# Moving the turn of x behind the value products in a pipelined transformer block

## The reference

```
tgt1 = layer_norm(tgt, g1, be1)
q, k, v = tgt1 @ Wq.T + bq, tgt1 @ Wk.T + bk, tgt1 @ Wv.T + bv
p = softmax(q k^T / 4 + (1 - mask) * -1e9)        # 16 heads
tgt = tgt + (p v) @ Wo.T + bo + memory @ Wg.T + bg
tgt1 = layer_norm(tgt, g2, be2)
return tgt + relu(tgt1 @ W1.T + b1) @ W2.T + b2
```

## Time and profile before

| | us |
|---|---|
| median of 3 runs | 1762.45 (1761.9 to 1763.15) |
| the profiled execution | 1762.95 |
| its span | 1761.2 |
| PE busy | 1723.3 (98%) |
| ScalarE busy | 1435.8 (82%) |
| VectorE busy | 1323.8 (75%) |
| GpSimd busy | 800.4 (45%) |

### The profile page before, as it was taken

How to read it: one execution, slowest core, us unless ns; L and a number is a source line. 1 busy time by engine, 2 the same in 40 slices (tenths; PEclk the granted TensorE clock), 3 DMA queues, 4 the chain that set the end, 5 groups by cost and what they waited for, 6 DMA issues and landing times.

```text
span 1761.2 us, 53553 instructions
## 1 busy us (share of the span) xinstructions
PE 1723.3 (98%) x17780; PEld 1696.0 (96%) x17780; DVE 1323.8 (75%) x6935; ACT 1435.8 (82%) x5577; POOL 800.4 (45%) x782
## 2 busy tenths in 40 slices
PE   5899999999999999999999999999999999999997
PEld 5799999999999999999999999999999999999997
DVE  7677777777777777777777777787777777777772
ACT  4888888888888888888888888888888888888882
POOL 4244444444444444444454454444444444444444
PEclk8899999999999999999999999999999999999999
DMA  5333333333333333333333333332433433433320
GB/s 169 109 127 107 115 123 108 117 121 107 120 121 106 121 120 107 122 118 109 121 118 103 127 112 105 131 118 95 134 116 96 135 113 100 134 112 103 126 80 25
DMA packets 185796, 200.46 MB, mean 114 GB/s; under 512 B 18864, under 2 KB 135984, under 8 KB 185520
## 3 DMA queue, kind: packets, MB, share of 16 engines
q1 hardware_dynamic: 185520, 197.02, 34.0%
HBM read 62.73 MB, written 16.78 MB: 45 GB/s over the span
## 4 chain that ended last, share of the span: by engine, by line
PE 95%; ACT 2%; DVE 1%; issue 0%; SPq 0%; DMA 0%; ACTq 0%; DVEq 0%
PE ffn_ps L808 13%; PE ffn_ps L810 13%; PE ffn_ps L809 13%; PE turn_ps L874 12%; PE work_ps L808 9%; PE work_ps L810 8%; PE work_ps L809 8%; PE score_ps L860 7%; PE value_ps L897 7%; PE work_ps L825 3%; ACT scores L388 1%; PE turn_ps L882 0%; ACT probs L400 0%; DVE xhat L556 0%; ACT hid L430 0%
## 5 line engine op out<-in xcount | busy, mean ns | idle before, releaser
L388 ACT ACTIVATE scores<-scores,row_min 128x128 f32<-128x128 f32 x2048 | 795.1, 402 | 2.3 <-DVE row_min L624 2.2
L738 POOL TENSOR_TENSOR hT_lo<-hid,hT_hi 128x512 fp32r<-128x512 f32 x256 | 355.0, 1387 | 511.9 <-DVE hT_hi L651 511.9
L624 DVE CUSTOM_DVE_ANT_0 scores<-score_ps,mask_bias 128x128 f32<-128x128 f32 x2048 | 472.4, 286 | 3.3 <-issue 2.9
L400 ACT ACTIVATE probs<-turn_ps 128x512 f32<-128x512 f32 x512 | 304.1, 595 | 163.0 <-PE turn_ps L874 163.0
L388 ACT ACTIVATION_READ_ACCUMULATOR scores<-scores,row_min 128x1 f32 x2048 | 411.1, 201 | 0.0
L874 PE MATMUL turn_ps<-ident,scores 128*128 128x128 f32 x2048 | 308.2, 273 | 5.3 <-ACT probs L400 5.2
L808 PE MATMUL ffn_ps<-zT_hi,w_lo 128*128 128x256 f32 x1024 | 302.2, 295 | 5.2 <-ACT hid L430 4.0
L808 PE MATMUL ffn_ps<-w_hi,hT_lo 128*128 128x256 f32 x1024 | 300.7, 294 | 2.4 <-ACT hid L430 2.4
L809 PE MATMUL ffn_ps<-zT_lo,w_hi 128*128 128x256 f32 x1024 | 285.5, 279 | 0.0
L810 PE MATMUL ffn_ps<-zT_hi,w_hi 128*128 128x256 f32 x1024 | 285.0, 278 | 0.0
L810 PE MATMUL ffn_ps<-w_hi,hT_hi 128*128 128x256 f32 x1024 | 284.7, 278 | 0.0
(11 more groups left out here) (112 smaller groups left out, 4187.1 us busy)
## 6 DMA issues: line engine op xcount, KB each, us to landing
q_stack<-q_hi SPq DMA_DIRECT2D x128, 256.0 KB, 2.4
k_stack<-k_hi SPq DMA_DIRECT2D x256, 128.0 KB, 2.3
x_in<-x_dram SPq DMA_DIRECT2D x64, 256.0 KB, 2.7
mem_in<-memory_dram SPq DMA_DIRECT2D x64, 256.0 KB, 3.3
x_res<-x_dram SPq DMA_DIRECT2D x64, 256.0 KB, 3.2
q_stack<-q_lo SPq DMA_DIRECT2D x64, 256.0 KB, 2.3
k_stack<-k_lo SPq DMA_DIRECT2D x128, 128.0 KB, 2.3
inv<-inv_cols SPq DMA_DIRECT2D x256, 64.0 KB, 2.1
```

Of the source, the lines that this page charges most:

```text
L388: last = act.activation(exps, exps, ACT.Exp, bias=row_min[:, k, h:h + 1], scale=-1.0, accum_out=row_sum[:, k, h:h + 1])
L400: act.activation(probs[:, k, :], turn_ps[k % 2][:, :], ACT.Copy).then_inc(probs_copied, 1)
L624: last = dve.tensor_tensor_reduce(out=scores[:, slot(i, t), h, :], in0=score_ps[t % 2][:, h * S:(h + 1) * S], in1=mask_bias[:, b, :], scal ...
L738: pool.tensor_tensor(halves[1], src, halves[0], ALU.subtract).then_inc(done, 1)
```

## The change

The x turn goes from tick 0 (between the turn of chunk 7 and up 0) to tick 1, behind the values. Up 1 and score 3 come from tick 2 to tick 1, between the x turn and the query product. So PE's order becomes: scores 0 and 1, turn of chunk 7, up 0 | score 2, values, x turn, up 1, score 3, query product | (nothing) | score 4, turn 0, key product.

The other engines follow. ScalarE makes xT_hi at tick 1, behind exponentials 0 and ReLU 0 and ahead of exponentials 1; q_hi stays at tick 2 but stands behind exponentials 2 instead of ahead of them (its lines move into a function `high_queries`). ReLU 1 stays at tick 3. VectorE makes xT_lo at tick 1, behind masks 1 and ahead of hT_hi 0, instead of behind masks 0. No instruction is added or removed, and no semaphore's count changes. The whole diff:

```diff
--- before.py
+++ after.py
@@ -37,8 +37,8 @@
 HIGHEST = 3.0e38
 
 TICKS = 13
-SCORE_TICKS = {2: 3, 3: 4, 5: 5, 6: 6, 7: 7}
-UP_TICKS = (0, 2, 4, 7)
+SCORE_TICKS = {3: 4, 5: 5, 6: 6, 7: 7}
+UP_TICKS = (0, 1, 4, 7)
 HIDDEN_TICKS = (1, 3, 5, 8)
 RELU_TICKS = (0, 3, 5, 7)
 DOWN_TICKS = (9, 10, 11, 12)
@@ -400,6 +400,18 @@
                 act.activation(probs[:, k, :], turn_ps[k % 2][:, :], ACT.Copy
                                ).then_inc(probs_copied, 1)
 
+            def high_queries(g):
+
+                if not later(g):
+                    act.wait_ge(shift_added, 2)
+                act.wait_ge(q_ready, g + 1)
+                if later(g):
+                    act.wait_ge(q_stacked, 16 * TERMS * g)
+                for k in range(KT):
+                    last = act.activation(q[0][:, k, :], by_tile[1][:, k, :], ACT.Identity,
+                                          bias=bqc[:, k:k + 1])
+                last.then_inc(q_high, 1)
+
             def copy_inverses(g):
 
                 act.wait_ge(inv_turned, g + 1)
@@ -411,10 +423,6 @@
                 for t in range(TICKS):
                     if out_ and t == 0:
                         copy_turned(i - 1, CHUNKS - 1)
-                    if front and t == 0:
-                        g = i + 1
-                        split_high(by_tile[1], xT[0], x_turned, g + 1, v_ready,
-                                   g if later(g) else None, x_hi)
                     if attn_ and t == EXP_TICKS[0]:
                         exponentials(i, 0)
                     if is_at(i, 2) and t == 0:
@@ -436,17 +444,6 @@
                         g = i - 1
                         split_high(by_tile[1], zT[0], z_turned, g + 1, hid_ready,
                                    HJ * g if later(g) else None, z_hi)
-                    if front and t == 2:
-                        g = i + 1
-                        if not later(g):
-                            act.wait_ge(shift_added, 2)
-                        act.wait_ge(q_ready, g + 1)
-                        if later(g):
-                            act.wait_ge(q_stacked, 16 * TERMS * g)
-                        for k in range(KT):
-                            last = act.activation(q[0][:, k, :], by_tile[1][:, k, :], ACT.Identity,
-                                                  bias=bqc[:, k:k + 1])
-                        last.then_inc(q_high, 1)
                     if front and t == 3:
                         g = i + 1
                         act.wait_ge(k_ready, g + 1)
@@ -456,8 +453,14 @@
                             last = act.activation(kk[0][:, k, :], by_tile[0][:, k, :], ACT.Identity,
                                                   bias=bkc[:, k:k + 1])
                         last.then_inc(k_high, 1)
+                    if front and t == 1:
+                        g = i + 1
+                        split_high(by_tile[1], xT[0], x_turned, g + 1, v_ready,
+                                   g if later(g) else None, x_hi)
                     if attn_ and t in EXP_TICKS[1:]:
                         exponentials(i, EXP_TICKS.index(t))
+                    if front and t == 2:
+                        high_queries(i + 1)
                     if attn_ and t == 12:
                         copy_inverses(i)
 
@@ -912,17 +915,21 @@
                         turn_chunk(i, TURN_TICKS.index(t))
                     if out_ and t == 0:
                         turn_chunk(i - 1, CHUNKS - 1)
-                    if front and t == 0:
-                        pe.wait_ge(ln1_ready, i + 2)
-                        if not isinstance(i, int) or outs > 0:
-                            pe.wait_ge(z_split, outs)
-                        turn(by_tile[1], xhat).then_inc(x_turned, 1)
-                    if ffn and t in UP_TICKS:
+                    if ffn and t in UP_TICKS and t != 1:
                         up(i, t)
                     if attn_ and t == 1:
                         scores_of(i, 2)
                     if out_ and t == 1:
                         values_of(i - 1)
+                    if front and t == 1:
+                        pe.wait_ge(ln1_ready, i + 2)
+                        if not isinstance(i, int) or outs > 0:
+                            pe.wait_ge(z_split, outs)
+                        turn(by_tile[1], xhat).then_inc(x_turned, 1)
+                    if ffn and t == 1:
+                        up(i, t)
+                    if attn_ and t == 1:
+                        scores_of(i, 3)
                     if front and t in (1, 3):
                         which = t // 2
                         if which == 0:
```

## The result

The changed kernel takes 1792.49 us (median of 4 runs, 1792.16 to 1793.31); the kernel before, run beside it on the same chip, 1762.8. The ratio is 1.0168, with a 95% interval of 1.0155 to 1.0181: slower by 1.7%. The profiled execution took 1792.77 us, its span 1791.0 against 1761.2 before. The forecast was 1792.0, in a range of 1776 to 1804.

A forecast was written before the change was run, and what follows sets the result against it. PE's own queue was taken as the bound, with matmuls in flight 98% of the span. 0.47 us an iteration, 61 times, gave 28.7, plus 1.2 for iterations 0 and 1: 1792 us for the median, range 1776 to 1804.

The forecast's parts named there:

- Step 1: PE, up 0 directly behind the turn of chunk 7: 0.45 us, the x turn's cover for y worth 0.09.
- Step 2: PE, x turn behind the values: 1.88 us after they start, plus 0.05 for late weights; starts 4.11 behind chunk 7's turn.
- Step 3: PE's own way from the x turn through up 1, score 3 and query product to up 2: 6.02 us.
- A: Rival: the cross-engine chain is shorter than summed and PE's own way decides; +0.10 us an iteration, 1770 us; chance 0.08.
- Step 4: Chain over ScalarE and VectorE from x turn to up 2: 6.37 us, so up 2 waits 0.35 an iteration.
- Late next: First output product on PE, waiting for q_lo: ready after 1.90 us, reached after 2.13, so it holds by about 0.2.
- The sum: Whole kernel: 0.47 us an iteration, 61 times, 28.7 us, plus 1.2 us for iterations 0 and 1.
- The start: Iterations 0 and 1, without feed-forward: xT_hi's 0.59 moves into ScalarE's work, twice, 1.2 us, between 0 and 2.5.
- B: Rival: x turn behind the values without emptying the array, q's weights loaded ahead; 0.08 us less an iteration, 1758; chance 0.05.
- C: Rival: a further wait, from slower hT_hi 0 or masks, or at the output product; 21 us more, 1813; chance 0.04.
- D: Rival: the order changes nothing PE feels, the waits being hidden; 1760 to 1765 us; chance 0.03.
- The signs: Profile after: 0.45 to up 0, 1.88 behind values, up 2 waits 0.3, VectorE idle 3, q_hi without bracket, stretch 10.5.

The follow-up runs named there:

- the chain cut on VectorE: Changed kernel with xT_lo on VectorE moved behind hT_hi 0 and the masks of chunk 2 from iteration 2 on: 1771.14 us, ratio 1.0046.
- both kernels show in which the chain was cut: Changed kernel with either xT_lo behind the masks of chunk 2 on VectorE (1771.14 us) or ReLU 1 at tick 2 on ScalarE (1770.71 us).
- the kernel with the chain lengthened: Changed kernel with q_hi on ScalarE put back ahead of the exponentials of chunk 2: 1828.01 us, ratio 1.0369.
- the kernel with the late query product alone: Changed kernel with the x turn, xT_hi and xT_lo back at tick 0, the rest of the change kept: 1764.2 us, ratio 1.0005.

## Why the prediction came out, step by step

**The bound.** PE's queue was the bound, and it still is but for the 0.38 us an iteration in which up 2 waits. No other engine had to become slower for that: they only had to be later.

**Step 1** said 0.45 from the turn of chunk 7 to up 0: 865.08 - 864.63 = 0.45. That the x turn covers 0.09 is shown by the kernel with the x turn back at tick 0, where up 0 follows its neighbour after 0.36 again. That it is y for which up 0 waits is read from the program and was not tested.

**Step 2** said 1.88 for the values and 0.05 for the x turn's late weights: 868.74 - 866.85 = 1.89 and 869.15 - 868.74 = 0.41, of which 0.05 is more than the usual 0.36. The x turn starts 4.11 behind the turn of chunk 7, as summed.

**Step 3** gave PE's own way from the x turn as 6.02. Up 2 could have started 0.35 behind the turn of chunk 1, 5.99 behind the x turn. The step has a slip: its own terms bring PE to the query product at 2.11, and yet it lets the product begin at 2.05; with 2.11 its sum is 6.08, which would have made A 10 us instead of 6 and the wait 0.29 instead of 0.35. The product started 2.10 behind the x turn. It did wait a little for x_split, as said: xT_lo ends at 870.06 + 0.69 = 870.75, and the first weight load, whose neighbours follow each other after 0.11, starts 0.20 behind the one at 870.61:

```profile
870.81 0.19 PEld L811 LDWEIGHTS work_ps<-xT_hi,wq_lo 128*128 128x128 f32 x1
```

The first matmul takes 0.36, where it takes 0.28 with the x turn back at tick 0 (855.96). The whole product took 1.45 and not 1.52, which made up for the slip. None of this decided anything, since the chain was longer.

**Step 4**, the term that decided, gave 6.37 from the x turn to up 2: 875.12 - 868.74 = 6.38. No link of the sum is off by more than 0.03. The wait was forecast at 0.35 and is 0.38. Late next was to be the output product, by a margin of 0.2: q_lo ends at 876.05 + 0.87 = 876.92, and the product starts at 877.19, 2.07 behind up 2, as when nothing waits.

**The sum** has two mis-sized terms, in opposite directions. An iteration costs 0.433 and not 0.47: the stretch is 0.46 longer, and 0.03 comes back behind it. In iterations 3 to 62 that makes 26.0 instead of 28.7 for 61 iterations. The start was put at 1.2, between 0 and 2.5, and is 3.9 (iterations 0 to 2), outside its own bounds. The step that failed is the reasoning that only ScalarE's 0.59 for xT_hi would move out of a pause. PE in iteration 0 of the kernel after:

```profile
36.69 1.06 PE L828 MATMUL work_ps<-ident,xhat 128*128 128x128 f32 x4
...
39.16 0.58 PE L811 MATMUL work_ps<-xT_hi,wq_lo 128*128 128x256 f32 x1 [0.99 <-DVE xT_lo L590]
```

and of the kernel before:

```profile
32.41 1.12 PE L825 MATMUL work_ps<-ident,xhat 128*128 128x128 f32 x4 [5.47 <-DVE xhat L556]
36.35 0.80 PE L860 MATMUL score_ps<-k_stack,q_stack 128*128 128x256 f32 x2 [2.83 <-DVE row_min L624]
36.96 0.58 PE L808 MATMUL work_ps<-xT_hi,wq_lo 128*128 128x256 f32 x1
```

Before, the x turn ran while PE had nothing else, and q was ready behind score 2. Now the x turn starts behind score 2, and without a feed-forward there is no up 1 between it and the query product, only score 3; the chain through xT_hi and xT_lo is bare, PE waits 0.99 for it, and q starts 2.2 later. Behind it ScalarE pauses ahead of q_hi (0.48), the copy of chunk 0 (0.44) and k_hi (1.17). In iteration 1 PE waits 1.17 for xT_lo at the same place. By the turns of the inverses (56.72, 79.65, 108.98 after; 54.29, 75.77, 105.13 before) 2.43 are lost up to the first, 1.45 up to the second, and iteration 2, counted among the 61, loses nothing.

TensorE's granted clock has a part in this start, which the forecast left out. It is at the lower of its two levels (0.50, that is 1.2 GHz) in both kernels when score 2 of iteration 0 starts, after PE has stood idle, for 9.22 us in the kernel after and for 5.47 and 2.83 us around the x turn before. While PE then works, it rises to 1.00, at 41 us before and at 44 after. The turn of chunk 0 and the key product lie there (stretch, us, busy us and instructions of each engine, granted clock, DMA share, GB/s), before:

```profile
40.54:42.54 2.00, 2.00 (x18) 2.00 (x18) 2.00 (x16) 2.00 (x10) 0.00 (x0) 0.91 0.00 0
```

and after:

```profile
42.31:44.96 2.65, 2.65 (x17) 2.65 (x17) 1.73 (x11) 1.25 (x3) 0.00 (x0) 0.67 0.01 3
```

These two blocks take 0.65 longer, which is that much of the 2.43, at the lower clock. In iteration 2 the mean clock is 0.90 before (75.77 to 105.13) and 0.94 after (79.65 to 108.98), which may hide the wait at up 2 there. With the chain cut on VectorE, where iterations 0 and 1 are those of the kernel after, iteration 3 opens at 107.70, 2.57 later than before and not 3.85; 0.46 of the difference is iteration 2's (28.87 against 29.33). The 3.9 are thus order and clock together, and no run parts them.

The first term was 2.7 too large and the second 2.7 too small, so that the forecast is closer to the time than its terms are.

**The rivals.** A, PE's own way deciding, was put at 1770. It is what both kernels show in which the chain was cut, 1771.14 and 1770.71: the right price for a case that did not occur. They are 8.2 and 7.8 over the kernel before. In their traces iteration 3 opens 2.6 and 2.8 later (107.70 and 107.95), and iterations 3 to 62 take 4.0 and 4.4 more, 0.07 each; A had 0.10 times 61 and 1.2, so it too is right by two errors. B, faster by an array that does not empty, falls with the 1.88 and 1.89 behind the values, whichever block follows. By "TensorEngine Tiling (Array Packing)", Key Properties, in the Trainium skill the change of tiling mode empties the engine. The three kinds of block that followed the values in these kernels, a turn, the query product and up 1 (854.20 - 852.32 = 1.88 with the x turn back at tick 0), agree with 1.88 to 1.89, where going on without a break was estimated at 1.79. No run here puts a block of the values' own tiling behind them. C, a second wait, did not come. D is out by 30 us.

**The signs.** Four came as said (0.45; 1.88; 10.5 for the stretch; q_hi without a bracket behind the exponentials), and VectorE's pause is 3.42 where 3 was named. One came elsewhere: "some 20 us in the list" of PE's waits stand in the list of its weight loads (+23.1), while PE's own line did not move. PE is counted as busy to the modelled end of a matmul's passage: the turn of chunk 1 is counted to 874.38 + 0.60 = 874.98, and of the 0.38 only 0.14 lie behind that, without a bracket in the row of up 2. In the kernel with the chain lengthened, where the wait is 0.89 at the weights, the bracket is there, 0.66 on PE. Whoever had looked for the wait in PE's line alone would have called the forecast refuted.

**Still open.** Why 0.03 comes back behind the stretch. Means over iterations 6 to 60 of both traces make it 0.02, half of it in up 2 itself (1.486 instead of 1.496) and half in the two scores behind it (0.228 instead of 0.237); the reason was not sought.

## What to carry to other kernels

Before an instruction is moved on the engine that bounds the kernel, write down, for each engine that follows it, what is queued behind the first wait that gets later, and add up that chain to the next thing the bounding engine needs; here it ran over three engines and eight pieces of work, and the plain durations of the old trace gave it to 0.01 us. A late wait on an engine with 25% idle time is cheap to mend, by one instruction moved behind it or ahead of it: here 21 of 30 us each. And cost the first iterations by themselves, since the work that covers a chain in the steady state is not there yet, and the granted clock may not be the same: here 0.50 in parts of iterations 0 to 2, 1.00 behind them.

## What the runs showed of the hardware that was not expected

A block of 12 equal matmuls runs at a slower or at a faster pace. In the kernel with the late query product alone, up 1 and the query product behind it (of each the fourth and the tenth of its twelve matmuls):

```profile
854.66 0.28 PE L810 MATMUL ffn_ps<-zT_hi,w_lo 128*128 128x256 f32 x1
...
855.37 0.28 PE L810 MATMUL ffn_ps<-zT_hi,w_lo 128*128 128x256 f32 x1
...
856.32 0.28 PE L810 MATMUL work_ps<-xT_hi,wq_lo 128*128 128x256 f32 x1
...
857.00 0.28 PE L810 MATMUL work_ps<-xT_hi,wq_lo 128*128 128x256 f32 x1
```

Six steps take 0.71 in up 1 and 0.68 in the query product, 118 and 113 ns from start to start; the granted clock is 1.00 in both stretches. It is no property of the block: in the kernel after, up 1 takes 0.68 for them (869.59 to 870.27), and before, the query product took 1.52 in all and in the kernel after 1.45. So a block that is only moved can change by 0.05 us, as much as some terms of this forecast. What sets the pace was not found, and no run was made for it.
